# Order of the twelve products in an even step of the down projection: accumulator by accumulator in place of all high parts first

## The chip, the cores and the metric

One NeuronCore of a Trainium2 chip runs the whole program. The metric is the device time of one execution in microseconds (us). Engines are named as the profile names them: PE is TensorE's matmul side, PEld its weight loads, DVE is VectorE, ACT is ScalarE, POOL is GpSimd, SP is SyncE.

## What is computed

A cross-attention layer and then a mixture of experts, all in float32:

```python
x = x + xattn(layernorm(x), ctx, W_k, b_k, gamma, beta)
# FFN over 8 experts, top 2 of them for each token:
h = ragged_dot(rows, w1, group_sizes)              # D=1024 -> M=3584
h = silu(h) * ragged_dot(rows, w3, group_sizes)
out_sort = ragged_dot(h, w2, group_sizes)          # M -> D, the down projection
out = einsum('tkd,tk->td', gathered(out_sort), topk_w)
x = x + out
```

## The kernel before

The attention and the routing come first and stay as they are. The rest is a loop over **slots**: a slot is one expert with up to 1088 of its rows. Eight slots run in this input. The rows of a slot stand in two halves, so a matmul streams one of eight widths; here two slots have width 496, two 512, one 544 and three 528. A width up to 512 is one matmul per product (one PSUM bank); 528 and 544 are two matmuls of 264 and 272 columns each.

Each float32 operand is split into a high and a low part (`wh`, `wl`), and a product is three matmuls: high x high, high x low, low x high. In the names of the trace the moving operand stands first: `pair<-wl,wh` streams the low part of the hidden values against the high part of the weights, `pair<-wh,wl` is the reverse, and `pair<-wh` has both high. Block products are made in Strassen's manner with 7 products for 8.

A slot has two phases. The first (28 units, line 1673) makes the hidden values and stores them to `hd` in DRAM. The second is the **down phase**: 7 passes (`p`) of 14 steps, two steps to an iteration of the loop over `i2`. The function `down` on PE makes one iteration: `par` 0 is the even step, `par` 1 the odd one. One step multiplies one 128-row block of w2 with one block of hidden values into four accumulators `pair[0]` to `pair[3]`: 4 accumulators x 3 matmuls, so 12 or 24 matmuls, all on line 1706, each with a weight load of its own.

Around it:

- SP loads w2 and hidden blocks (`raw2`, `rawh`) up to three steps ahead. ACT makes the high parts (line 1088) and DVE the low parts (line 1313), into buffers that step t shares with step t-2. ACT starts on step t when `s_down` says that all four accumulators of step t-2 have had their last matmul; PE starts step t when `s_w2lo` and `s_hlo` say that DVE has made both low parts (lines 1702 and 1703).
- Between two passes the accumulators are emptied by ACT and DVE (`results_out`), then PE transposes into the same PSUM banks: input rows for the next slot (`turn_rows`, line 1752, ahead of passes 0 to 4 but 2), a tail (`turn_tail`, line 1761, ahead of pass 3), or the finished results (`turn_back`, line 1771, ahead of passes 2, 5 and 6 and at the slot's end). ACT and DVE drain them again; DVE's `scaled_rows` is line 1534. The first step of a pass (`i2 == 0`, even) waits for each accumulator's `s_acc[d]` before its first matmul.
- The code of `down` stands eight times in PE's program, once for each width, and `by_width` (line 1735) branches to the one that is wanted in each iteration. The end of the loop over `i2` is line 1798.

Of the kernel before, what the change touches and what calls it, by code (L numbers as in the profile page):

```python
# [855 lines left out]
def experts(nc, w1, w3, w2, out, x2_rows, table, meta, raw13, s_raw13):  # L856

    with ExitStack() as st:
        def sb(name, shape, dt=F32):
            return st.enter_context(nc.sbuf_tensor(name, shape, dt))  # L860

        def sem(name):
            return st.enter_context(nc.semaphore(name))
# [6 lines left out]
        wh = sb("wh", [P, EP * KH * P], F32R)  # L870
        wl = sb("wl", [P, EP * KH * P], F32R)
# [74 lines left out]
        s_down = sem("s_down")  # L946
# [45 lines left out]
        def down_w(w, par):  # L992
            return w[:, par * HALF:(par + 1) * HALF]

        def down_h(w, par):
            return w[:, 2 * HALF + par * COLS:2 * HALF + (par + 1) * COLS]
# [659 lines left out]
        def _(pe):  # L1656
            def parts_of(n):

                return [(0, 0, n)] if n <= BANK else [(0, 0, n // 2), (1, n // 2, n)]
# [37 lines left out]
            def down(s, p, i2, n):  # L1697

                for par in range(2):
                    t = s * STEPS + p * PAIRS + i2 * 2 + par  # L1700
                    pe.wait_ge(s_w2lo, t + 3)
                    pe.wait_ge(s_hlo, t + 3)

                    def part_of(d, w, h, begin=False, end=False):
                        for ch, lo, hi in parts_of(n):
                            mm = pe.matmul(pair[d][:, ch, 0:hi - lo], down_w(w, par)[:, d * P:(d + 1) * P],  # L1706
                                           down_h(h, par)[:, lo:hi], start=begin, stop=end, skip_group_check=True)
                        return mm

                    if par == 0:  # L1710
                        with pe.If(i2 == 0):
                            pe.wait_ge(s_c11, s * UNITS2 + UNITS2 + 1)
                            pe.wait_ge(s_c12, s * UNITS2 + UNITS2 + 1)
                            pe.wait_ge(s_c21, s * UNITS2 + UNITS2 + 1)
                            for d in range(4):
                                pe.wait_ge(s_acc[d], s * EVENTS + 2 + 2 * p)
                                part_of(d, wh, wh, begin=True)
                        with pe.Else():
                            for d in range(4):
                                part_of(d, wh, wh)  # L1720
                    for d in range(4):
                        if par == 1:
                            part_of(d, wh, wh)
                        part_of(d, wh, wl)
                        mm = part_of(d, wl, wh, end=True)
                        mm.then_inc(s_down, 1)

            def by_width(width, body):

# [55 lines left out]
            def slot(s, width):  # L1785
# [11 lines left out]
                with pe.Fori(0, EP) as p:  # L1797
                    with pe.Fori(0, PAIRS // 2) as i2:
                        by_width(width, lambda n: down(s, p, i2, n))

                    def evicted(q):
                        pe.wait_ge(s_acc[q], s * EVENTS + 3 + 2 * p)

                    with pe.If(p > 3):
                        turn_back(s, p, p - 3, width)
                    with pe.Else():
                        with pe.If(p == 1):
                            turn_back(s, p, 0, width)
                        with pe.Else():
                            with pe.If(p == 0):  # L1810
                                turn_rows(xg, 1, evicted, s_xg, s * 128 + 64)
                            with pe.Else():
                                turn_rows(xg, 1, evicted, s_xg, s * 128 + p * 32 + 32)
                                with pe.If(p == 2):
                                    turn_tail(s_acc[1], s * EVENTS + 4 + 2 * 2, s_xgt, s * 16 + 16)
                                    pe.wait_ge(s_tq, s + 2)
                                    pe.nop()
                                pe.nop()
                            pe.nop()
                        pe.nop()  # L1820
                    pe.nop()

            pe.wait_ge(s_ident, 2)
            for i in range(8):
                for j in range(4):
                    mm = pe.transpose(pair[i // 2][:, i % 2, j * P:(j + 1) * P], ident[:, :], ident[:, :])
# [197 lines left out]
```

## Time and profile before

| | us |
|---|---|
| median of 3 runs | 7891.59 (7889.98 to 7897.8) |
| the profiled execution | 7890.05 |
| its span in the trace | 7888.4 |
| PE busy | 7419.7 (94%) |
| PEld busy | 6607.3 (84%) |
| DVE busy | 5038.4 (64%) |
| ACT busy | 2871.2 (36%) |

Mean granted TensorE clock of the profiled execution: 0.97. In a timeline the first number is the start in us from the span's start, the second the time that the group takes, `xN` how many instructions were merged, and the bracket the engine's idle time before the group with what ended it. The distance between two starts is the time that lies between them; the ends of matmuls are modelled.

### The profile page before, as it was taken

The page shows a single profiled execution, that of the slowest core. Times are in us where ns is not written, and L with a number is a line of the kernel's source. Part 1 is how long each engine was busy: PE and PEld are TensorE (multiplying, and loading weights), DVE is VectorE, ACT ScalarE, POOL GpSimd, SP SyncE. Part 2 cuts the span into 40 slices and gives each one's busy share as a digit, 9 for nine tenths or more (in the row PEclk, how much of TensorE's full clock was granted, in tenths as well). Part 3 has the DMA queues.
Part 4 walks back from the last instruction along what each step waited for, and adds up shares of the span by engine and source line. Part 5 has one row for each costly group of instructions (what it writes and reads, how often), then busy time and mean ns, then how long its engine had stood idle before and what let it go on. Part 6 is the DMA issues. An engine that isn't in the chain of part 4 may idle for free.

```text
span 7888.4 us, 139188 instructions
## 1 busy us (share of the span) xinstructions
PE 7419.7 (94%) x45405; PEld 6607.3 (84%) x45406; DVE 5038.4 (64%) x8017; ACT 2871.2 (36%) x4875; POOL 907.7 (12%) x1344
## 2 busy tenths in 40 slices
PE   8968999899989999899999999899998999999998
PEld 4547887788779999888778999878778999999997
DVE  6767765577556665577656665577655665566655
ACT  2323334333443334333343334433343333433343
POOL 2330011100110010100111001100101001010011
PEclk9969999999999999999999999999999999999999
DMA  3333456544654445544564445544564445544455
GB/s 117 108 100 131 166 174 189 158 166 161 193 177 145 141 156 178 153 159 160 178 196 135 146 147 184 165 156 156 173 186 143 155 141 178 181 138 145 150 182 159
DMA packets 683953, 1247.67 MB, mean 158 GB/s; under 512 B 50528, under 2 KB 286448, under 8 KB 683632
## 3 DMA queue, kind: packets, MB, share of 16 engines
q1 hardware_dynamic: 584240, 935.24, 35.9%
q0 software_dynamic: 99392, 309.05, 12.3%
q8 instruction: 92, 1.51, 0.1%
q14 instruction: 229, 1.88, 0.1%
HBM read 840.81 MB, written 405.38 MB: 158 GB/s over the span
## 4 chain that ended last, share of the span: by engine, by line
PE 84%; DVE 3%; issue 3%; DMA 1%; ACT 1%; DVEq 0%; SPq 0%; POOL 0%; ACTq 0%; POOLq 0%
PE pair L1673 57%; PE pair L1706 26%; DVE wl L1313 1%; PE pair L1771 1%; DVE sil L1316 1%; DMA raw<-hd 1%; ACT wh L1088 1%; PE pair L1752 0%; DMA xg<-w2s 0%; DVE hid L1316 0%; DVE sil L1534 0%; DVE sil L1313 0%; DVE xl L1313 0%; ACT part L1088 0%; DVE part L1316 0%
## 5 line engine op out<-in xcount | busy, mean ns | idle before, releaser
L1673 PE MATMUL pair<-xh,wh 128*128 128x264 f32 (+3 forms) x9408 | 2517.0, 322 | 103.0 <-issue 82.6
L1673 PE MATMUL pair<-xh,wl 128*128 128x264 f32 (+3 forms) x9408 | 2525.4, 323 | 13.7 <-issue 13.7
L1673 PE MATMUL pair<-xl,wh 128*128 128x264 f32 (+3 forms) x9408 | 2515.4, 322 | 0.0
L1313 DVE TENSOR_TENSOR wl<-raw,wh 128x512 fp32r<-128x512 f32 (+2 forms) x1875 | 1259.8, 692 | 1102.8 <-ACT wh L1088 1089.9
L1673 PEld LDWEIGHTS pair<-xh,wh 128*128 128x128 f32 x9408 | 1584.4, 190 | 242.7 <-issue 120.0
L1673 PEld LDWEIGHTS pair<-xh,wl 128*128 128x128 f32 x9408 | 1577.2, 189 | 142.5 <-issue 14.6
L1673 PEld LDWEIGHTS pair<-xl,wh 128*128 128x128 f32 x9408 | 1573.5, 189 | 122.5
L1088 ACT ACTIVATE wh<-raw 128x512 fp32r<-128x512 f32 (+2 forms) x1875 | 1134.7, 628 | 1443.0 <-PE pair L1706 710.2
L1706 PE MATMUL pair<-wh,wl 128*128 128x264 f32 (+3 forms) x4704 | 1264.1, 323 | 0.0
L1706 PE MATMUL pair<-wl,wh 128*128 128x264 f32 (+3 forms) x4704 | 1264.0, 323 | 0.0
L1706 PE MATMUL pair<-wh 128*128 128x264 f32 (+3 forms) x4704 | 1093.5, 328 | 120.8 <-issue 75.0
L1088 ACT ACTIVATE wh<-sums 128x512 fp32r<-128x512 f32 x900 | 566.2, 631 | 1547.4 <-PE pair L1673 1520.5
L1706 PEld LDWEIGHTS pair<-wh 128*128 128x128 f32 x4704 | 745.3, 191 | 220.5 <-issue 123.4
L1706 PEld LDWEIGHTS pair<-wl,wh 128*128 128x128 f32 x4704 | 794.1, 191 | 63.8 <-issue 0.3
L1852 POOL TENSOR_TENSOR ticks<-ticks 128x1 f32<-128x1 f32 x316 | 115.5, 365 | 6359.9 <-DVE xg L1313 3271.1
L1706 PEld LDWEIGHTS pair<-wh,wl 128*128 128x128 f32 x4704 | 792.9, 191 | 63.7
L1313 DVE TENSOR_TENSOR wl<-sums,wh 128x512 fp32r<-128x512 f32 x900 | 616.6, 687 | 206.0 <-ACT wh L1088 197.6
L1316 DVE TENSOR_TENSOR part<-part,pair 128x512 f32<-128x512 f32 (+2 forms) x448 | 312.6, 698 | 469.9 <-PE pair L1673 469.9
L1313 DVE TENSOR_TENSOR wl<-part,wh 128x512 fp32r<-128x512 f32 (+1 forms) x272 | 186.8, 692 | 402.9 <-ACT wh L1088 401.4
L1088 ACT ACTIVATE wh<-part 128x512 fp32r<-128x512 f32 (+1 forms) x272 | 170.4, 631 | 465.0 <-PE pair L1706 464.9
L1091 ACT ACTIVATE sil<-sil 128x512 f32<-128x512 f32 (+2 forms) x336 | 215.5, 641 | 272.3 <-DVE sil L1316 261.1
L1316 DVE TENSOR_TENSOR sil<-part,pair 128x512 f32<-128x512 f32 (+2 forms) x368 | 253.4, 692 | 36.9 <-PE pair L1673 33.7
(253 smaller groups left out, 5499.1 us busy)
## 6 DMA issues: line engine op xcount, KB each, us to landing
raw<-in_L_ffn_w SPq DMA_DIRECT2D x226, 1024.0 KB
raw<-hd SPq DMA_DIRECT2D x720, 272.0 KB
hd<-hid SPq DMA_DIRECT2D x112, 1088.0 KB, 4.4
hd<-sil SPq DMA_DIRECT2D x112, 816.0 KB, 6.8
raw<-w2s SPq DMA_DIRECT2D x256, 256.0 KB
w2v<-in_L_ffn_w POOLq DMA_DIRECT2D x112, 512.0 KB, 3.6
xg<-in_L_ffn_w POOLq DMA_DIRECT2D x112, 512.0 KB, 4.4
w2s<-w2v POOLq DMA_DIRECT2D x112, 512.0 KB, 5.3
```

The costliest lines, as they stand in the source:

```text
L1088: return nc.scalar.activation(out, in_, ACT.Copy)
L1091: return nc.scalar.activation(out, in_, ACT.Silu)
L1313: return V.tensor_tensor(out, a, b, ALU.subtract)
L1316: return V.tensor_tensor(out, a, b, ALU.add)
L1673: mm = pe.matmul(to[:, c, 0:hi - lo], entry(w, e)[:, ks], x[:, e, k, lo:hi], start=begin and k == 0 and i == 0, stop=k == KH - 1 and i == ...
L1706: mm = pe.matmul(pair[d][:, ch, 0:hi - lo], down_w(w, par)[:, d * P:(d + 1) * P], down_h(h, par)[:, lo:hi], start=begin, stop=end, skip_gr ...
L1771: mm = pe.transpose(o, yT[:, d, j * P:j * P + r], ident[:, :])
L1852: G.tensor_tensor(ticks[:, 0:1], ticks[:, 0:1], ticks[:, 1:2], ALU.add).then_inc(s_tick, 1)
```

## The change

In the even step, the three matmuls of an accumulator now follow each other, in both branches: in the first step of a pass (behind that accumulator's wait) and in every other even step. Before, the high x high matmuls of all four accumulators came first and the other two kinds afterwards. The odd step had this order already and keeps it. The shared second half of the even step is now written into both branches.

```diff
+                    def rest(d):
+                        part_of(d, wh, wl)
+                        mm = part_of(d, wl, wh, end=True)
+                        mm.then_inc(s_down, 1)
+
                     if par == 0:
                         with pe.If(i2 == 0):
...
                             for d in range(4):
                                 pe.wait_ge(s_acc[d], s * EVENTS + 2 + 2 * p)
                                 part_of(d, wh, wh, begin=True)
+                                rest(d)
                         with pe.Else():
                             for d in range(4):
                                 part_of(d, wh, wh)
-                    for d in range(4):
-                        if par == 1:
+                                rest(d)
+                        pe.nop()
+                    else:
+                        for d in range(4):
                             part_of(d, wh, wh)
-                        part_of(d, wh, wl)
-                        mm = part_of(d, wl, wh, end=True)
-                        mm.then_inc(s_down, 1)
+                            rest(d)
```

PE's program for width 512 before, from the start of the even step: the branch on `i2 == 0`, the wait, four high x high matmuls, the jump over the other branch, the other branch's four, and the shared rest.

```order
L1711 COMPARE_AND_BRANCH
L1716 ISA
L1706 MATMUL pair<-wh 128x512 x4
L1711 UNCONDITIONAL_BRANCH
L1706 MATMUL pair<-wh 128x512 x4
L1718 UNCONDITIONAL_BRANCH
L1706 MATMUL pair<-wl,wh 128x512
L1706 MATMUL pair<-wh,wl 128x512
L1706 MATMUL pair<-wl,wh 128x512
L1706 MATMUL pair<-wh,wl 128x512
```

The same place in the changed program, from the last accumulator of the first branch on:

```order
L1706 MATMUL pair<-wh 128x512
L1706 MATMUL pair<-wl,wh 128x512
L1706 MATMUL pair<-wh,wl 128x512
L1716 UNCONDITIONAL_BRANCH
L1706 MATMUL pair<-wh 128x512
L1706 MATMUL pair<-wl,wh 128x512
L1706 MATMUL pair<-wh,wl 128x512
L1706 MATMUL pair<-wh 128x512
L1706 MATMUL pair<-wl,wh 128x512
L1706 MATMUL pair<-wh,wl 128x512
```

The same 12 matmuls are executed, but each branch holds all of them. The program has 8 more matmuls in the code of each of the six widths up to 512 and 16 more in that of 528 and 544: 80 in all, each with its weight load. DVE's, ACT's, POOL's and SP's instructions don't move.

## Rows read from the trace of the kernel before

**Rows 1.** The page's chain of waits: shares of the span by engine and by line.
```profile
PE 84%; DVE 3%; issue 3%; DMA 1%; ACT 1%; DVEq 0%; SPq 0%; POOL 0%; ACTq 0%; POOLq 0%
PE pair L1673 57%; PE pair L1706 26%; DVE wl L1313 1%; PE pair L1771 1%; DVE sil L1316 1%; DMA raw<-hd 1%; ACT wh L1088 1%; PE pair L1752 0%; DMA xg<-w2s 0%; DVE hid L1316 0%; DVE sil L1534 0%; DVE sil L1313 0%; DVE xl L1313 0%; ACT part L1088 0%; DVE part L1316 0%
```
**Rows 2.** PE's waits: waited for, us in total, times, longest.
```profile
PE pair L1706 <- issue: 75.0, 27, 6.3
PE pair L1706 <- DVE sil L1534: 20.3, 24, 0.8
```
**Rows 3.** Timeline, weight loads, start of pass 1, width 496.
```profile
2060.39 0.75 PEld L1706 LDWEIGHTS pair<-wh 128*128 128x128 f32 x4 [1.72 <-issue]
```
**Rows 4.** Timeline, weight loads, start of pass 5 in that slot.
```profile
2238.26 0.30 PEld L1706 LDWEIGHTS pair<-wh 128*128 128x128 f32 x2 [1.08 <-DVE sil L1534]
2238.91 0.30 PEld L1706 LDWEIGHTS pair<-wh 128*128 128x128 f32 x2 [0.36 <-DVE sil L1534]
```
**Rows 5.** Timeline, PE, starts of passes 1 and 5, width 528.
```profile
6643.01 1.22 PE L1706 MATMUL pair<-wh 128*128 128x264 f32 x8 [1.39 <-issue]
...
6830.99 1.41 PE L1706 MATMUL pair<-wh 128*128 128x264 f32 x8 [0.84 <-DVE sil L1534]
```
**Rows 6.** Timeline, weight loads, first two iterations of pass 0, widths 496 and 528.
```profile
1147.58 0.52 PEld L1706 LDWEIGHTS pair<-wh 128*128 128x128 f32 x3 [0.29 <-issue]
1149.52 0.19 PEld L1706 LDWEIGHTS pair<-wh 128*128 128x128 f32 x1 [1.42 <-issue]
...
1157.35 0.52 PEld L1706 LDWEIGHTS pair<-wh 128*128 128x128 f32 x3 [3.15 <-issue]
...
4773.43 0.72 PEld L1706 LDWEIGHTS pair<-wh 128*128 128x128 f32 x3 [6.46 <-issue]
```
**Rows 7.** DMA view of 4764 to 4774: load of the queues.
```profile
q1 hardware_dynamic: 1208, 2.37, 62.8%
q0 software_dynamic: 368, 1.31, 37.7%
q8 instruction: 1, 0.02, 0.6%
```
**Rows 8.** Timeline, PE, an even and an odd step, width 528.
```profile
6672.36 1.15 PE L1706 MATMUL pair<-wh 128*128 128x264 f32 x8
6673.35 0.40 PE L1706 MATMUL pair<-wl,wh 128*128 128x264 f32 x2
...
6675.27 0.41 PE L1706 MATMUL pair<-wh 128*128 128x264 f32 x2
...
6678.23 0.40 PE L1706 MATMUL pair<-wh 128*128 128x264 f32 x2
```
**Rows 9.** The same, an odd and then an even step, width 512.
```profile
3904.00 0.40 PE L1706 MATMUL pair<-wh 128*128 128x512 f32 x1
...
3906.80 1.09 PE L1706 MATMUL pair<-wh 128*128 128x512 f32 x4
...
3909.55 0.40 PE L1706 MATMUL pair<-wh 128*128 128x512 f32 x1
```
**Rows 10.** The same, even then odd, width 544.
```profile
2996.31 1.17 PE L1706 MATMUL pair<-wh 128*128 128x272 f32 x8
...
2999.34 0.41 PE L1706 MATMUL pair<-wh 128*128 128x272 f32 x2
...
3002.34 0.92 PE L1706 MATMUL pair<-wh 128*128 128x272 f32 x6
```
**Rows 11.** The same, even then odd, width 496, with the weight load that opens it.
```profile
2071.20 1.13 PE L1706 MATMUL pair<-wh 128*128 128x496 f32 x4
...
2073.96 0.39 PE L1706 MATMUL pair<-wh 128*128 128x496 f32 x1
...
2076.66 0.66 PE L1706 MATMUL pair<-wh 128*128 128x496 f32 x2
...
2071.17 0.74 PEld L1706 LDWEIGHTS pair<-wh 128*128 128x128 f32 x4 [0.21 <-issue]
```
**Rows 12.** Timeline, PE, 24 matmuls of one product in the first phase, width 528.
```profile
6300.19 0.41 PE L1673 MATMUL pair<-xh,wh 128*128 128x264 f32 x2
...
6303.15 0.41 PE L1673 MATMUL pair<-xh,wh 128*128 128x264 f32 x2
```

## The prediction

> **What bounds the kernel.** I read the page's chain of waits first. PE carries 84% of it, 57% on line 1673 and 26% on line 1706, the down phase [rows 1]. So PE's time there counts one for one, unless something behind it absorbs a change. Next the list of PE's waits: line 1706 stands idle for DVE's `scaled_rows` 24 times, which is 8 slots by the three passes 2, 5 and 6 that follow `turn_back`, and 75.0 us in 27 waits on nothing that the profile shows, up to 6.3 us at a time [rows 2]. Then the timeline at four kinds of places: a pass start without a late accumulator, one with, the first iterations of pass 0, and plain even and odd steps in the middle of a pass. The reader is to look there at starts and their distances, since matmul ends are modelled.
>
> The change touches every even step, 49 in a slot and 392 in all. No DMA is moved, and no engine but PE gets other instructions. I take the even step apart into where it starts a pass and what it costs everywhere.
>
> **Pass starts, passes 2, 5 and 6.** `scaled_rows` frees accumulators 0 and 2 on DVE one after the other. In an undisturbed start the four opening weight loads take 0.75 us [rows 3]. Behind `turn_back` they stand in two pairs with 0.36 us idle between them, from 2238.26 to 2238.91 + 0.30 = 2239.21, so 0.95 us: 0.20 us lost [rows 4]. At width 528 the opening eight matmuls take 1.41 us against 1.22: 0.19 us lost [rows 5]. In the new order the third accumulator is needed only after six matmuls of width 496, well over 1 us after the start, and DVE frees it 0.65 us after the start [rows 4]. So the wait goes. 12 x 0.20 + 12 x 0.19 = 4.7 us gained. Passes 1, 3 and 4 have no such gap: nothing there. What is late next is step 2, whose split starts when step 0 is complete, so it moves along with step 0 and the gain is kept. The gain can't be more than this by that mechanism, and at starts that run at the low clock it can be less: I take 4.7, bounds 3 to 5.
>
> **Pass starts, pass 0.** Here ACT copies all four quadrants out one after the other, and accumulator 3 comes late: in the first slot its weight load starts at 1149.52 after 1.42 us idle [rows 6]. In the new order nine matmuls stand ahead of it in place of three. Six more at (2073.96 - 2071.20)/12 = 0.23 us [rows 11] are 1.4 us, so nearly all of that wait would be covered. But two steps later PE stands again, until 1157.35, after 3.15 us without work, and in a 528 slot for 6.46 us [rows 6]. The trace has a block of instructions arriving in the longer of these gaps, on the queue q8, while data packets fill 62.8% and 37.7% of the DMA engines' time [rows 7]. I read it as PE's branch to the end of the loop waiting for code that isn't on the core yet. When that wait begins is set by the sequencer, which runs ahead of PE; finishing step 0 earlier then only lengthens the gap. I keep 1.0 us for all eight slots, some 0.1 us each, because the sequencer is released a little earlier. Bounds: from nothing to all, 1.4 us in each of eight slots, would be 0 to 11; but the low end needs the code wait to move along fully.
>
> The Trainium skill, "Runtime: NRT & Kernel Launch", section "Instruction fetch mechanics", says that code comes in 16 KiB blocks and that a taken branch to a block not on the chip stalls until it has been fetched; the rows agree as far as one such block lies in the gap.
>
> **Every even step.** The change makes the even step's order that of the odd step, so the odd step prices it. Width 528: the even step takes 6675.27 - 6672.36 = 2.91 us, the odd one behind it 6678.23 - 6675.27 = 2.96 us [rows 8]. Within the even step the eight high x high matmuls take 0.99 us, 0.124 each, and the remaining 16, in which high x low and low x high alternate, take 1.92 us, 0.120 each [rows 8]. 24 matmuls of the first phase, which has the triplet order too and always the same accumulator, take 6303.15 - 6300.19 = 2.96 us [rows 12], the odd step's length. So it seems to be the order that costs, not the buffers or the accumulators: 0.05 us a step, 3 slots x 49 x 0.05 = 7.4 us lost. Width 512: odd 3906.80 - 3904.00 = 2.80, even 3909.55 - 3906.80 = 2.75 [rows 9]; 2 x 49 x 0.05 = 4.9 us lost. Width 544: even 3.03, odd 3.00 [rows 10]; 49 x 0.03 = 1.5 us gained. Width 496: even 2.76, odd 2.70 [rows 11], but this even step opens with 0.21 us without a weight load, since PE gets there as the split is just finished and has the branch still to take. That belongs to the place, not to the order, and stays; I take zero, bounds -0.06 to +0.02 us a step, so -6 to +2 us over 98 steps. Sum of the even steps: 7.4 + 4.9 - 1.5 + 0 = 10.8 us lost. Bounds: zero, if the lengths go with the place, and 13.
>
> [...]
>
> **The rest of the change.** `s_down` now rises after every third matmul in the even step too, but ACT waits for the fourth rise of a step, which comes with the last matmul as before: nothing. The extra `nop`: PE's sequencer is ahead of PE there; if that cover were gone it would be a fraction of the 0.21 us that the opening of an even step shows [rows 11].
>
> **Sum.** 10.8 - 4.7 - 1.0 = +5.1 us. The profiled execution took 7890.05 us, so 7895.2; the median of the runs is 1.5 us above it, so 7891.59 + 5.1 = 7896.7 us. One thing that the sum leaves out is the clock: it is granted at 0.97 of the full rate on the whole, and short stretches at half of it follow the gaps of pass starts. Whether a gap is a little shorter or longer can switch one on or off, a microsecond or two each, in either direction.
>
> **Rivals.**
>
> *A, the order costs nothing.* The lengths of even and odd steps could come from the place: different halves of the buffers, or what DVE and ACT write meanwhile. Against it: the first phase has the odd step's pace in quite another place [rows 12]. For it: width 544 goes the other way [rows 10], which a cost of the order alone would not lead one to expect. Then only the starts count: 7891.59 - 5.7 = 7885.9 us.
>
> *B, slower: a new wait for code.* The eight copies of `down` grow by 80 matmuls and their weight loads. The bodies of widths 512 and 496 stand behind those of 544 and 528, so they move furthest from the loop's head that branches to them. If they come to lie in a block that isn't there when pass 0 of a slot begins, PE waits once more: for one block, 3.15 to 6.46 us [rows 6]. In the four slots of these widths that is 13 to 26 us, of which the waits for accumulator 3 hide 1.4 us each where they were; with 5 us net in each, 7896.7 + 20 = 7916.7 us. It decides the sign against the measurement from 10.7 us on top of the forecast, so from 2.7 us net in each of the four slots. For it: such waits exist in every slot. Against it: the block behind the head's is read ahead while PE waits for accumulators, and the odd steps then run from what is there. Within the passes nothing can be fetched again and again, or PE would stand in every iteration now.
>
> *C, faster: pass 0 keeps all.* If the gap after the second step is a wait for data that moves with step 0, pass 0 gives up to 11 us and the order costs nothing: 7885.9 - 10 = 7875.9 us. Against it: the gap in the 528 slot is 6.46 us with the operands' split not named as the cause [rows 6].
>
> *D, nothing moves*, because what the starts give the steps take: 7891.6 us.
>
> **Chances.** About 0.2%, 15.8 us, is what a measurement of this kernel can tell from no change. Forecast 0.58, range 7892 to 7902. A 0.20. B 0.13. C 0.03. D 0.06. Only C at its end is faster than 7875.8, with some luck with the clock in A: faster 0.03. B lies above 7907.4 in most of its range, and a part of the forecast's tail too: slower 0.13. Same 0.84. The range reaches from below A, 7884, to the middle of B, 7911.
>
> **What would show it.** Right: even and odd steps at 528 both 2.96 us apart, at 512 both 2.80; the opening loads of passes 2, 5 and 6 without the pause of 0.36 us and without DVE's `scaled_rows` as the cause of a second wait; the code gap of pass 0 where it was and longer, by about what its start gained. Wrong: even steps still at 2.91 us (A); a new idle stretch of 3 us or more ahead of the first matmul of pass 0 at 496 or 512, with a block on q8 in it (B); the gap after step 1 gone or moved forward with step 0 (C).

## The result, and the profile after

| | before | changed |
|---|---|---|
| median, us (22 runs each) | 7889.59 (7874.41 to 7898.64) | 7879.91 (7869.17 to 7891.92) |
| ratio | | 0.9988, 95% interval 0.9982 to 0.9993 |
| profiled execution, us | 7890.05 | 7886.34 |
| its span, us | 7888.4 | 7884.7 |

The changed kernel is 9.7 us faster (interval 5.5 to 14 us: the ratio's ends times 7889.59). I had forecast 5.1 us slower. That is 0.12%, less than the 0.2% that I had called measurable, but 22 runs resolve it, and it came out the same way twice more (0.9987 and 0.9981, below). It also lies under the low end of my wide range, 7884. Of all executions that are compared below one (of the kernel before, 8967.21 us) ran in a slower state of the chip, at a granted clock of 0.77; it is left out.

Lines of the changed kernel behind line 1712 stand 6 further down than before (`turn_rows` 1758, `turn_back` 1777); line 1706 is where it was. First its chain of waits and PE's waits, against [rows 1, 2]:

```profile
PE 84%; issue 3%; DVE 3%; DMA 1%; ACT 1%; POOL 0%; DVEq 0%; SPq 0%; POOLq 0%; ACTq 0%
```
```profile
PE pair L1673 <- issue: 89.0, 16, 15.3
PE pair L1706 <- issue: 67.2, 27, 6.5
PE pair L1706 <- DVE wl L1313: 31.3, 26, 4.7
PE pair L1706 <- DVE sil L1534: 20.3, 24, 0.8
```

PE's waits for nothing that the profile shows have shrunk on both lines: from 75.0 to 67.2 us on line 1706, and on line 1673, which the diff doesn't touch, to 89.0. The rows that they answer to are these of the kernel before:

```profile
PE pair L1673 <- issue: 96.3, 18, 16.0
PE pair L1706 <- DVE wl L1313: 25.3, 26, 2.0
```

On line 1706 the waits for DVE's `wl` have grown from 25.3 to 31.3 us meanwhile, so "issue" and `wl` together fell by 1.8 us only (100.3 to 98.5): the same pauses come under another label. In the third slot, for one, a pause of 6.1 us without a releaser ahead of step 2 of pass 0 has given way to one of 4.7 us for `wl` ahead of step 3.

The wait of 20.3 us for `scaled_rows` is unchanged. It is the one for accumulator 0, 0.84 us at a time; the pause that the change was to remove had been too short to be listed.

**The pass start.** Weight loads at the start of pass 5, second slot, width 496, against [rows 4]:

```profile
2236.53 0.19 PEld L1706 LDWEIGHTS pair<-wh 128*128 128x128 f32 x1 [1.08 <-DVE sil L1534]
2236.64 0.19 PEld L1706 LDWEIGHTS pair<-wl,wh 128*128 128x128 f32 x1
2236.87 0.19 PEld L1706 LDWEIGHTS pair<-wh,wl 128*128 128x128 f32 x1
2237.09 0.19 PEld L1706 LDWEIGHTS pair<-wh 128*128 128x128 f32 x1
...
2237.76 0.19 PEld L1706 LDWEIGHTS pair<-wh 128*128 128x128 f32 x1
```

Accumulator 2's first load comes 1.23 us after the start (2237.76 - 2236.53), and no pause stands before it.

**The steady steps.** PE, pass 1, width 528, against [rows 8]. An even step starts at the first of these rows, its ninth matmul at the second, the odd step at the third and the next even one at the fourth; between them the program's new order can be seen in the full timeline, `wh`, `wl,wh`, `wh,wl` four times:

```profile
6649.94 0.40 PE L1706 MATMUL pair<-wh 128*128 128x264 f32 x2
...
6650.93 0.40 PE L1706 MATMUL pair<-wl,wh 128*128 128x264 f32 x2
...
6652.85 0.41 PE L1706 MATMUL pair<-wh 128*128 128x264 f32 x2
...
6655.81 0.40 PE L1706 MATMUL pair<-wh 128*128 128x264 f32 x2
```

The even step takes 2.91 us and the odd one 2.96 us, as before. The order has not moved them. Nor has it moved the pace within the step: the first eight matmuls, now of all three kinds, take 0.99 us (6650.93 - 6649.94), as the eight high x high ones did [rows 8]. Over all plain steps of the down phase the median distances are, before and after alike: 2.906 and 2.961 us (even, odd) at width 528, 2.744 and 2.796 at 512, 3.030 and 3.003 at 544, and within 0.002 us of 2.723 and 2.702 at 496.

**Pass 0.** Weight loads in the first slot, against [rows 6]:

```profile
1141.46 0.86 PEld L1758 LDWEIGHTS pair<-ident,xg 128*128 128x128 f32 x8 [2.17 <-issue]
...
1146.35 0.19 PEld L1706 LDWEIGHTS pair<-wh 128*128 128x128 f32 x1 [3.16 <-issue]
...
1153.99 0.19 PEld L1706 LDWEIGHTS pair<-wh 128*128 128x128 f32 x1 [0.84 <-issue]
```

This is rival B's signature: 3.16 us without work ahead of the first load, where 0.29 us stood. It is there in the two slots of width 496, not in those of 512. But the pause of 1.42 us for accumulator 3 is gone, and the later gap is 0.84 us in place of 3.15 (one of 1.58 us for DVE's `wl` follows it). The pause for accumulator 3 had stood in these two slots only, not in all eight.

**Somewhere else.** One more place differs in every pair of traces: the third slot's first phase (width 544), 168 matmuls after its start, in the kernel before.

```profile
2354.49 0.41 PE L1673 MATMUL pair<-xh,wl 128*128 128x272 f32 x2
2358.08 0.52 PE L1673 MATMUL pair<-xh,wh 128*128 128x272 f32 x2 [3.18 <-issue]
```

The DMA view of that stretch (2354 to 2358.5) has two blocks of instructions in it:

```profile
q8 instruction: 2, 0.03, 2.7%
```

In the changed kernel a pause of 0.88 us for an accumulator is all that is left behind the phase's start:

```profile
2352.49 0.51 PE L1673 MATMUL pair<-xh,wh 128*128 128x272 f32 x2 [0.88 <-DVE sil L1316]
```

So three theories were to be told apart. **T**: only the starts of passes gain, by 4 to 6 us, and the order is free elsewhere. **The prediction's theory**: the order costs 10.8 us in the even steps. **L**: the gain comes from where the longer code comes to lie.

### The profile page after: what moved, and what is told of

Read it like the earlier page. It is cut to its first block, busy times and chain, and to the rows that moved or that the text cites. A ratio compares the mean times of both kernels' runs of the same rounds, so it can differ in the third digit from the quotient of the medians.

```text
span 7884.7 us, 139188 instructions
## 1 busy us (share of the span) xinstructions
PE 7420.7 (94%) x45405; PEld 6614.7 (84%) x45406; DVE 5039.0 (64%) x8017; ACT 2871.8 (36%) x4875; POOL 909.5 (12%) x1344
## 4 chain that ended last, share of the span: by engine, by line
PE 84%; issue 3%; DVE 3%; DMA 1%; ACT 1%; POOL 0%; DVEq 0%; SPq 0%; POOLq 0%; ACTq 0%
PE pair L1673 56%; PE pair L1706 26%; DVE wl L1313 1%; PE pair L1777 1%; DVE sil L1316 1%; DMA raw<-hd 1%; ACT wh L1088 1%; PE pair L1758 0%; DMA xg<-w2s 0%; DVE hid L1316 0%; DVE sil L1534 0%; DVE sil L1313 0%; POOL out_x L1895 0%; DVE xl L1313 0%; ACT part L1088 0%
## 5 line engine op out<-in xcount | busy, mean ns | idle before, releaser
L1706 PE MATMUL pair<-wh 128*128 128x264 f32 (+3 forms) x4704 | 1280.9, 327 | 119.3 <-issue 67.2
L1706 PEld LDWEIGHTS pair<-wh 128*128 128x128 f32 x4704 | 795.0, 191 | 220.6 <-issue 120.2
```

## The experiments

All of them are compared with the kernel before on the same chip; medians are in us. "Half clock" is TensorE's lower level, 1.2 GHz, which the profile shows as a granted clock of 0.5 in short stretches. Where I say "half clock taken out", half of such a stretch's length is subtracted; that is an estimate from those two levels.

### The four corners of the change

In all of them the second half of the even step is written into both branches, as in the changed kernel. Only the place of the inner loop differs; with `for d in range(4):` ahead of `rest(d)` a branch has the old order:

```diff
                             for d in range(4):
                                 pe.wait_ge(s_acc[d], s * EVENTS + 2 + 2 * p)
                                 part_of(d, wh, wh, begin=True)
+                            for d in range(4):
                                 rest(d)
                         with pe.Else():
                             for d in range(4):
                                 part_of(d, wh, wh)
+                            for d in range(4):
                                 rest(d)
```

Both additions: code only. The second alone: new order at the starts only. The first alone: new order in the rest only. Neither: the changed kernel.

Code only: 

> Old order everywhere; only the shared second half of the even step is written into both branches, so PE's code has the changed kernel's size. Theory T (the gain comes from the pass starts, the order itself costs nothing): no gain, within 2 us of the kernel before, and the starts of passes 2, 5 and 6 keep the pause between the second and third accumulator. Rival L (the gain comes from where the code lies and how long PE waits for it): this kernel has all of the changed kernel's gain, -6 to -13 us, and the same new waits at the start of pass 0 in the slots of width 496. Rival C (the difference is half-clock stretches that come and go): anything, and it will not repeat.

Starts only: 

> The new order only in the first step of a pass; every other even step keeps the old one; code size as in the changed kernel. Theory T: all of the gain, -5 to -10 us. The theory of the prediction (the new order costs 10.8 us in the even steps and the starts give back 5.7 us): -5.7 us, and the changed kernel would have been 10.8 us slower than this one. The step lengths in the trace decide between the two: T has 2.91 us for an even step of width 528 in both kernels.

Rest only: 

> The new order only in the even steps that do not start a pass; the starts keep the old one. Theory T: no difference, within 2 us of the kernel before, even steps at 2.91 us (width 528) and 2.75 us (width 512). The theory of the prediction: +10.8 us, even steps at 2.96 and 2.80 us.

And a kernel with the old order everywhere, the odd step included (the same edit in the last branch too): 

> The odd step gets the old order too (all four high x high products first), as the even step has before. If the order sets a step's length, the odd steps of width 528 fall from 2.96 to 2.91 us and those of width 512 from 2.80 to 2.75 us, 245 steps x 0.05 = 12 us faster. If the place sets it (theory T), the odd steps stay at 2.96 and 2.80 us and the time stays within 2 us of the kernel before. Rival P: an odd step that finishes its first accumulator later frees nothing later, since ACT waits for the fourth; so no loss is expected from that side.

The results left the time open, so the corners were run again together, on another chip. Code only: 

> Old order everywhere with the changed kernel's code size, again. If the code's size alone brings part of the gain, it lies 3 to 7 us under the kernel before; if not, within 2 us of it.

Starts only: 

> New order in the first steps of the passes only, again. Step 0 of passes 2, 5 and 6 is 3.7 us shorter in the traces of all kernels that have it: 3 to 8 us under the kernel that has only the code size.

Rest only: 

> New order in the other even steps only, again. Its first result, 12 us under the kernel before, was lower than theory T allows. By T it equals the kernel that has only the code size, within 3 us; if it is again 8 us or more below that one, something in the steady even steps brings a gain that the step lengths don't show.

The changed kernel: 

> The changed kernel a third time: 8 to 12 us under the kernel before. By theory T as fast as the one with the new order in the starts only, within 3 us.

| | first, before 7889.04 | ratio | again, before 7892.93 | ratio |
|---|---|---|---|---|
| code only | 7884.01 | 0.9996 (0.9986 to 1.0005) | 7883.93 | 0.9989 (0.9981 to 0.9998) |
| starts only | 7882.94 | 0.9995 (0.9984 to 1.0006) | 7880.78 | 0.9985 (0.9977 to 0.9994) |
| rest only | 7874.78 | 0.9985 (0.9974 to 0.9996) | 7882.69 | 0.9989 (0.9980 to 0.9998) |
| changed kernel | | | 7876.81 | 0.9981 (0.9972 to 0.9990) |
| old order everywhere | 7882.04 | 0.9994 (0.9984 to 1.0003) | | |

The ratio is an estimate of its own, not the quotient of the two medians, and the interval belongs to it. Single executions of one kernel lie 13 to 33 us apart from lowest to highest, so single medians decide little. Read together they say this. By its medians the code alone is 5.0 and 9.0 us under the kernel before, and the kernel with the old order everywhere 7.0; by the ratios it is 3.2, 8.7 and 4.7 us, and only the second of these intervals leaves out 1. So the sign is the same three times out of three, with no order in these kernels that the traces show to gain, but the size is loose: some 3 to 9 us. T had allowed 2 us. The new order at the starts adds 1.1, 3.1 and 5.9 us to that (code to starts, twice; rest to changed kernel). The new order in the rest adds 9.2, 1.2 and 4.0 (code to rest, twice; starts to changed kernel). Its first value was not repeated and the intervals don't separate the other two from nothing; T's bound for it, 2 us in the first comparison, was broken, and the traces show no step that became shorter.

The clock accounts for a good part of that 9.2. Each execution is on record with its span and its mean granted clock, and the span times the clock is an estimate of the time with all half clock taken out. Against the kernel before, the means of this product are lower by 4.6 and 6.7 us for code only, 4.1 for the old order everywhere, 5.1 and 4.0 for starts only, 7.2 and 4.3 for rest only, and 4.7 and 7.8 for the two repeats of the changed kernel, each with a standard error of about 2 us. By it rest only lies 2.6 us under code only in the first comparison (7.5 by the plain means) and 2.4 above it in the second. The code's part is there in all of them; a further part of either order can't be told from nothing by the times.

The traces settle the steps. Rest only, two whole steps of pass 1, width 528, first rows of each step:

```profile
6632.48 0.40 PE L1706 MATMUL pair<-wh 128*128 128x264 f32 x2
...
6635.38 0.41 PE L1706 MATMUL pair<-wh 128*128 128x264 f32 x2
...
6638.34 0.40 PE L1706 MATMUL pair<-wh 128*128 128x264 f32 x2
```

Even 2.90, odd 2.96. And an odd step in the old order (old order everywhere, the same step), eight high x high matmuls first:

```profile
6646.08 1.15 PE L1706 MATMUL pair<-wh 128*128 128x264 f32 x8
...
6649.04 0.40 PE L1706 MATMUL pair<-wh 128*128 128x264 f32 x2
```

Still 2.96. The order costs nothing in either direction that the step lengths show, and the 12 us of gain that the prediction's theory expected of this last kernel didn't come.

The first steps of passes 2, 5 and 6, 24 of them, with half clock taken out, sum to 72.5 to 73.3 us in the seven traces with the old order at the starts and the code of all widths (mean 73.0) and to 69.0 to 69.9 in the five with the new one (mean 69.5). The two groups don't touch: 3.5 us. (The traces with the delay or with other buffers, below, are in neither group.)

A part of the code's share can be read in PE's waits. The sum of the rows "issue" on lines 1673 and 1706 is 171.3 us before (96.3 + 75.0), and in the five traces with the longer code and the old order at the starts 154.0 to 159.7. Most of that fall is a change of label: with the waits for `wl` counted in, the two lines have 196.6 us before (190.6 in the repeat below) and 186.7 to 192.9 in the five, some 4 us less in the mean. For instance in the trace of code only:

```profile
PE pair L1673 <- issue: 90.9, 16, 15.2
PE pair L1706 <- issue: 68.8, 29, 6.0
```

### The same two kernels once more

The kernel before: 

> The kernel before once more, unchanged: what two runs of one kernel differ by. Ratio 1 within 0.1%. Its trace tells which of the differences between two traces come and go: theory T has the steps' time with the half-clock stretches taken out (half of their length subtracted) within 2 us of the first trace's 2534.0 us, while the number of those stretches differs by up to 8.

The changed kernel: 

> The changed kernel once more. Ratio 0.998 to 0.9995. Theory T: the steps' time without half-clock stretches again 2526 to 2528 us, 7 to 8 us under the kernel before. If that sum comes out at 2530 us or more, the difference of the first pair of traces was chance too.

Before again: 7888.38 against 7885.64 in its own comparison, ratio 1.0002 (0.9993 to 1.0011). Its trace has 168.6 us of "issue" on the two lines, the pause in the third slot's first phase again (3.0 us), and no late first load in pass 0. So these three belong to the shorter code and are not chance. The changed kernel again: 7874.76, ratio 0.9987 (0.9978 to 0.9996). The sum over the eight down phases, from the last transpose ahead of the first step to the end of the last step, half clock taken out, was 2529.2 us (before) and 2522.7 (changed); that is 6.5 us apart, but the repeats of the corners had 2525.3 (code only), 2533.0 (starts only), 2529.2 (rest only) and 2534.2 (changed kernel). I had expected this sum to hold within 2 us for one kernel and so to separate the two. It doesn't: it scatters by 10 us and is not used. The two repeats of the changed kernel lay 10.9 and 16.1 us under the kernel before; for the second I had expected 8 to 12.

### The wait doubled

```diff
                 for j in (0, 2):
+                    if j == 2:
+                        V.tensor_reduce(free_at_start[:, 12:13], ident[:, :].unsqueeze(1).to_broadcast([P, 12, P]),
+                                        AX.XY, ALU.max)
                     dve.wait_ge(s_yt, s * 20 + 5 * k + (j + 2 if k == 3 else 5) + 5)
```

On the kernel before: 

> The kernel before with one idle-work reduction on DVE (12 x 128 elements, about 1.6 us) between its two scaled_rows at the pass starts, so that accumulators 2 and 3 come later by that much at 24 (or, in the last drain of a slot, 32) places. Old order: each of the 24 starts of passes 2, 5 and 6 loses the whole delay, +30 to +45 us.

On the changed kernel: 

> The changed kernel with the same delay on DVE. New order: six matmuls stand ahead of the third accumulator, 1.4 us, and DVE was 0.65 us after the start, so 0.75 us of the delay is covered: the start loses about 0.85 us in place of 1.6, +15 to +25 us in all. If the new order did not move the need for accumulator 2, it loses as much as the old one, +30 to +45 us.

Against 7897.8 before: 7955.46 (ratio 1.0073, 1.0057 to 1.0088) and 7901.74 (1.0009, 0.9999 to 1.0018). The two rows of PE's waits, the kernel before with the delay and then the changed one with it (line 1709 is their line 1706):

```profile
PE pair L1709 <- DVE sil L1537: 57.1, 48, 1.6
```
```profile
PE pair L1709 <- DVE sil L1537: 31.4, 42, 0.8
```

And the weight loads at the start of pass 5, second slot, old order:

```profile
2250.10 0.30 PEld L1709 LDWEIGHTS pair<-wh 128*128 128x128 f32 x2 [1.08 <-DVE sil L1537]
2252.42 0.30 PEld L1709 LDWEIGHTS pair<-wh 128*128 128x128 f32 x2 [2.02 <-DVE sil L1537]
...
2253.61 0.33 PEld L1709 LDWEIGHTS pair<-wh,wl 128*128 128x128 f32 x1
```

New order:

```profile
2243.39 0.19 PEld L1709 LDWEIGHTS pair<-wh 128*128 128x128 f32 x1 [1.08 <-DVE sil L1537]
...
2245.70 0.19 PEld L1709 LDWEIGHTS pair<-wh 128*128 128x128 f32 x1 [1.13 <-DVE sil L1537]
```

The third accumulator is waited for 2.02 us in the old order and 1.13 in the new, 0.9 us less, against some 0.2 without the delay. The mechanism at the starts is shown. The new order with the delay is 3.9 us above the kernel before, so 14 to 20 above the changed kernel by the latter's distance in its three comparisons: about the 15 to 25 that I expected. The delaying instruction runs 32 times, also in each slot's last drain, where no first step follows. The price of the delay in the old order, 57.7 us, is above what I expected: the first steps of the 24 passes took 83.0 us before and 145.6 with the delay, 62.6 more, and only 35.4 of these remain when half clock is taken out. In the new order they took 98.4. Two windows of that start in the old order show why (the third figure from the end of a row is the granted clock):

```profile
2250.00:2253.40 3.40, 1.70 (x6) 1.17 (x7) 2.37 (x3) 0.57 (x1) 0.20 (x1) 0.97 0.26 91
2253.40:2256.80 3.40, 3.40 (x10) 2.68 (x10) 0.00 (x0) 0.40 (x1) 3.02 (x2) 0.53 0.37 37
```

PE did 1.70 us of work around its pause, and behind it the granted clock is 0.53. Over all 24 first steps the time at half clock was 20 us before, 26 with the delay in the new order, and 74 with it in the old one.

### Less code in the loop

PE's program gets code for the widths 496 to 544 only, the four that this input uses. The text below says "the down phase's code", but `by_width` serves the first phase (line 1673) as well, so the edit halves the code of both. A slot of a smaller width would run as one of 496, which was not tried:

```diff
+PE_WIDTHS = WIDTHS[-4:]
...
-                        body(WIDTHS[lo])
+                        body(PE_WIDTHS[lo])
```

On the kernel before: 

> The kernel before, but PE's program holds the down phase's code for the four largest widths only (496, 512, 528, 544; this input uses no other), so the whole loop is about half as long. If the idle time that the page puts to 'issue' in the first steps of pass 0 and at the loop's branches is a wait for code, most of the 75 us on line 1706 goes and the time falls by 20 to 100 us. If it is something else (a semaphore from an engine that the trace doesn't name), the gaps stay and the time stays within 5 us.

On the changed kernel: 

> The changed kernel with the same cut of the code. Theory T (the change gains only at the starts of passes 2, 5 and 6): 4 to 6 us less than the same cut of the kernel before, and nothing more, since no code wait is left for the change to move. Rival L (most of the gain is where the code lies): the difference between the two cut kernels is below 5 us and the changed kernel's further gain is gone. A wait of accumulator 3 in pass 0 (1.4 us a slot) may now come forward: with it the difference could reach 15 us.

Against 7897.8: 7836.0 (ratio 0.9926, 0.9913 to 0.9940) and 7837.31 (0.9928, 0.9915 to 0.9942), 62 and 60 us faster. PE's waits on the same two lines (now 1707 and 1674), the cut kernel before:

```profile
PE pair L1707 <- DVE wl L1314: 63.0, 38, 5.7
PE pair L1707 <- issue: 30.0, 13, 3.0
PE pair L1674 <- issue: 11.8, 4, 4.3
```

Of 171.3 us of "issue" 41.8 are left. So the rest was waiting for code, as I had read [rows 6], and not in pass 0 alone; the blocks on the queue q8 fall from 92 to 38 as well, here the row of the cut kernel:

```profile
q8 instruction: 38, 0.62, 0.0%
```

A part came back as waits for DVE's low part `wl`, 63.0 us in place of 25.3: at a slot's first steps the data was hardly earlier than the code. In pass 0 the stretches at half clock also shrink, from 40.8 us to 10.5 between the first phase's last matmul and step 3.

Most of the gain is elsewhere. From the end of one slot's last step to the first matmul of the next slot's first phase, seven times, PE needed 84.4 us before and needs 43.1 in the cut kernel; these are 41 of the 62 us, and they lie where PE enters the first phase's code, with waits of up to 16.0 us before. The way from the first phase's last matmul to step 3 fell from 159.3 to 142.0 us. By span times granted clock the cut kernel is 29 us under the kernel before, so about half of what was measured is clock (0.973 against 0.969). The edit also takes a comparison out of each pass through `by_width`; that this costs nothing in the steady steps is shown by their lengths, 2.906 and 2.961 us at width 528 as before. Of the 41.8 us that stay, most stand at the starts of passes 1, 3 and 4 (1.4 to 3.0 us each), and whether these are waits for code stays open.

The Trainium skill, "Runtime: NRT & Kernel Launch", section "Instruction fetch mechanics", has such a stall at a taken branch whose target isn't on the chip; the trace agrees, with the waits of 0.9 to 16 us that go when the code gets shorter.

Between the two cut kernels no difference can be measured, in five runs each. The starts' 4 to 6 us of T are neither shown nor excluded by the times; that the changed kernel's further gain vanishes fits L. In the traces the starts' gain is there (72.5 us for the 24 first steps, half clock taken out, and 69.5 with the new order), but the second trace has 64.4 us of "issue" on the two lines and 47 blocks on q8, against 41.8 and 38: where the code lies still differs between the two, so they don't compare the orders alone.

### Which place sets a step's length

Both halves of the operand buffers swapped between even and odd steps, on the changed kernel (with ACT's waits adjusted to it):

```diff
-            return w[:, par * HALF:(par + 1) * HALF]
+            return w[:, (1 - par) * HALF:(2 - par) * HALF]
...
-            return w[:, 2 * HALF + par * COLS:2 * HALF + (par + 1) * COLS]
+            return w[:, 2 * HALF + (1 - par) * COLS:2 * HALF + (2 - par) * COLS]
```

> The changed kernel with the two halves of the operand buffers swapped: even steps read the half that odd steps read, and the reverse. If the buffers' place sets the lengths, they swap: 2.96 us for an even step of width 528 and 2.91 for an odd one, 2.80 and 2.75 at width 512. If the code's place on PE or what the other engines do meanwhile sets it, they stay at 2.91 and 2.96. The time: within 8 us of the changed kernel either way, since even and odd steps are equally many; ACT waits a little longer before the first loads of a slot.

The lengths swapped. Even, odd, even step of pass 1, width 528:

```profile
6663.72 0.41 PE L1706 MATMUL pair<-wh 128*128 128x264 f32 x2
...
6666.68 0.40 PE L1706 MATMUL pair<-wh 128*128 128x264 f32 x2
...
6669.59 0.29 PE L1706 MATMUL pair<-wh 128*128 128x264 f32 x1
```

2.96 and 2.91. The length goes with the buffer's place. The time was 7906.63 (ratio 1.0029, 1.0018 to 1.0040), 21 us slower than the kernel before and outside what I expected. The width 496 explains 3.4 us (2.778 + 2.683 against 2.723 + 2.703, 98 pairs); the trace shows two places at which most of the rest is lost. From a slot's last step to the next slot's first phase PE needs 101.2 us where the changed kernel has 83.5, which the kernel with only the weights swapped has as well (101.3), and the way to the first steps of pass 0 is 44.7 us in place of 36.4. Both are places at which ACT's waits were adjusted.

Then one operand at a time. Only the odd step's hidden values moved, from byte 6272 of the buffer to 8192:

```diff
-            return w[:, 2 * HALF + par * COLS:2 * HALF + (par + 1) * COLS]
+            return w[:, (2 + 2 * par) * HALF:(2 + 2 * par) * HALF + COLS]
```

> The changed kernel with the odd step's hidden values 8192 bytes into the buffer in place of 6272 (the even step's stand at 4096; the weights stay where they are). If the moving operand's address sets the length, an odd step now has the even step's: 2.91 in place of 2.96 us at width 528, 2.75 in place of 2.80 at 512, 3.03 in place of 3.00 at 544; in all 147 x 0.055 + 98 x 0.05 - 49 x 0.03 = 11.5 us faster than the changed kernel. If the weights' address sets it, nothing changes.

Only the weights swapped: 

> The changed kernel with the weights of even and odd steps swapped and the hidden values left alone, the other half of the swap of both. If the weights' address sets the length, even steps of width 528 take 2.96 and odd ones 2.91 us; if the moving operand's does, they stay at 2.91 and 2.96.

All together: 

> All that helped together: the changed kernel, the down phase's code for the four largest widths only, and the odd step's hidden values at 8192 bytes. If the moving operand's address sets the length, 7837 - 11.5 = 7826 us; if not, 7837 us as without it.

With the weights swapped (one run, 7896.04, from which no time is read), the step at 6657.47 is followed by those at 6660.37 and 6663.33: 2.90 and 2.96, nothing moved. With the odd hidden values moved:

```profile
6625.88 0.40 PE L1706 MATMUL pair<-wh 128*128 128x264 f32 x2
...
6628.76 0.40 PE L1706 MATMUL pair<-wh 128*128 128x264 f32 x2
...
6631.64 0.40 PE L1706 MATMUL pair<-wh 128*128 128x264 f32 x2
```

2.88 and 2.88. So the place of the hidden values counts, and more than I expected: the even step got shorter too, though its own operand stayed where it was. A step's own operand therefore doesn't set its length alone. What ACT and DVE write during the even step, the odd step's hidden values, moved with the edit; whether the reading or the writing matters was not told apart. At width 512 the medians are 2.759 and 2.722 us (2.744 and 2.796 before), at 544 3.040 and 3.040 (3.030 and 3.003), at 496 2.747 and 2.683. The time: 7868.01 against 7891.53, ratio 0.9971 (0.9961 to 0.9980), 23.5 us under the kernel before, where the changed kernel lay 9.7, 10.9 and 16.1 us under it; the step lengths alone give 19.2 (147 x 0.107 at 528, 98 x 0.059 at 512, less 49 x 0.047 at 544). Some 13 us of that are lost again in pass 0, whose way to step 0 is 56.0 us in place of 36.4 (to step 3 169.0 in place of 156.1); in this edit ACT's copy of the first odd step's values waits for a product more of the first phase (idle 4.71 us ahead of it in place of 2.04 in the first slot), and DVE stands behind it.

All together: 7816.39, ratio 0.9902 (0.9887 to 0.9917). I had expected 7826. This beats both kernels, by 75 and some 60 to 65 us.

## Why the prediction was wrong

**The step that failed** is "every even step": "So it seems to be the order that costs, not the buffers or the accumulators", 10.8 us lost. It was nothing. I took a difference between two kinds of step for the price of the one property that I wanted to know, while they differed in the buffers' place too. The first phase's 2.96 us [rows 12] was no second witness, as it has another place as well; and width 544 with the opposite sign [rows 10] was the sign that I had even written down against it. The 0.124 and 0.120 us that I read for high x high and for the other products [rows 8] went by the position in the step: in the new order the first eight matmuls take 0.99 us too. Rival A had this right. The Trainium skill, "TensorE: Matmul & The Clock Gate", section "Back-to-back issue gap", gives for an isolated warm matmul N/2.4 + 2.5 ns, a time that goes by its columns alone; for 264 columns that would be 112.5 ns, an estimate from the page's figure. The traces agree in that the order costs nothing, and differ in the size and in the place: 0.120 to 0.123 us for the same 264 columns in this stream, each with a weight load.

**The code's place was missing from the sum**, except as rival B, with the wrong sign. B's new wait came in two of its four slots: in those of width 496 the first load of pass 0 comes 2.8 us later, and the way to step 0 grows from 30.8 to 36.4 us over the eight slots (it is 30.7 to 30.9 in all three traces with the code of the kernel before, 36.2 to 37.0 in the eleven with the longer code and the buffers where they were). I priced the wait that appears, and not what goes with it. To step 3 the eight slots took 159.3, 162.1 and 160.8 us with the short code, and 155.8 to 159.0, mean 157.3, with the longer code and the old order at the starts: 3.4 us less in spite of the new wait. These 3.4 us are the clock's: the time at half clock on this way is 40.8 to 50.2 us with the short code and 32.2 to 37.0 with the longer, and with it taken out the way is 135.7 to 138.9 us against 138.4 to 140.5, so rather longer. And in the third slot's first phase 3.1 us go (592.3 to 593.2 us with the short code, 589.0 to 590.6 with the longer, half clock taken out). Together 6.5 us of gain, about what code only measured, 5.0 and 9.0 by the medians. Why this pause goes and the half clock shrinks when the code gets longer was not tested; that the blocks' limits fall elsewhere is my reading.

**Pass starts 2, 5 and 6**: forecast 4.7, bounds 3 to 5; it is 3.5. The mechanism is as told. Where no half clock falls into it, the first step of these passes went from 3.00 to 2.79 us at width 496, from 3.09 to 2.87 at 512, from 3.17 to 3.00 at 528 and from 3.28 to 3.13 at 544, which over 24 starts would be 4.6 us; the sum over all of them, half clock taken out, has 3.5, so the starts with half clock gain less, as the prediction allowed.

**Pass 0's start**: forecast 1.0, with a bound of 11 that took the pause for accumulator 3 to be in all eight slots, where it was in two; with the same code the way to step 3 is 156.6 us (mean of six traces) with the new start order against 157.3: 0.7, well inside the scatter.

**The sum as it should have stood**, put together after the runs: 0 for the steps, -3.5 and -0.7 for the starts, -6.5 for the code: -10.7 us, against 9.7, 10.9 and 16.1 us between the medians of the three comparisons. That it comes out so near is in part luck, since the places of the code's part were picked with the result known. What I said of the clock holds for one stretch (the shortest are 3.4 us long, so cost 1.7), but many come and go: over the down phases the traces of the kernels with all widths and no delay have 103 to 143 us at half clock, 119.4 in the first trace of the kernel before and 136.5 in that of the changed one. That is why the first pair of traces shows no gain in the sum of the down phases with nothing taken out (2593.7 and 2594.7 us), where the runs do.

Still open: whether the new order in the steady steps has a gain of its own of a microsecond or two, which the step lengths don't show; and why the address of one step's operand also changes the pace of the other step.

## What to carry to other kernels

When two places of a kernel differ in several things, their difference prices none of them; look for a third place that differs in one thing only, and take a sign that goes the other way seriously. A change that lengthens an engine's loop moves every branch target behind it: where the loop waits for code, count the waits that go as well as those that come, under all their labels, and see first whether code that is not needed can leave the loop, which was worth 60 us here, six times the change. Needing an accumulator later is cheap insurance: it was worth 3.5 us as the kernel stood, and the two orders lay 54 us apart when the engine that frees it was 1.7 us late.

## What the runs showed of the hardware

- The pace of matmuls depends on where the hidden values, the moving operand, lie: 24 matmuls of 264 columns take 2.961 us in the step whose values lie at byte 6272 of the buffer and 2.906 in the one with 4096, and 2.880 in both kinds of step once the odd one's lie at 8192. At 272 columns the order is reversed (3.003, 3.030, 3.040). The weights' place had no such effect, nor had the order of the products. Since the even step changed with the odd one's values, it is not the place of a step's own operand alone; the mechanism was not found.
- With the loop's code halved, 130 of 171 us of PE's waits without a named releaser went, single ones of 0.9 to 16 us, mostly where a slot's two phases begin; 38 us came back as waits for DVE's `wl`. The time fell by 60 us, about half of it by the granted clock (0.969 to 0.973).
- With a second pause of 2.02 us at 24 pass starts PE ran 74 us of the first steps at half clock, with one of 1.13 us 26, and with one of 0.36 us or less 20. So the same delay on DVE, 1.7 us, cost 57.7 us in the old order, of which some 35 were the wait.
